# Attention maxima from queries and keys split into high and low parts instead of plain fp32 ones

## The chip, the cores and the metric

The kernel runs on one core of one Trainium2 chip, as one program. The metric is the time on the device in microseconds (us). Engine names in the profile: PE is TensorE (PEld its weight loads), DVE is VectorE, ACT is ScalarE, POOL is GpSimd, SP is SyncE, which issues DMAs.

## The reference, cut to what matters

```python
# b = 16 batches of 128 query rows, 2048 keys, 16 heads of 32
x = x + xattn(layernorm(x), ctx, ctx, wq, bq, wk, bk, wv, bv, wo, bo)
x = x + attn(layernorm(x), ...)     # causal linear attention and an MLP
x = x + ffn(layernorm(x), ...)      # linears with blockwise fp4 values

def xattn(q, k, v, wq, bq, wk, bk, wv, bv, wo, bo):
    qh, kh, vh = split into heads (q @ wq + bq), (k @ wk + bk), (v @ wv + bv)
    score = softmax(qh @ kh.T / sqrt(32), axis=-1)     # over the 2048 keys
    return (score @ vh) @ wo + bo
```

The change lies in the first line, in the cross attention. A softmax may subtract any number that is near the largest score of the row from all scores of that row. The kernel computes the scores twice: once with queries on the output partitions, to take the maximum over the keys, and once with keys on the partitions, with the maximum subtracted, for the exponential.

## The kernel before, in words

Everything is in one block with one program per engine; each engine works through its own program in order and waits on semaphores. The kernel first projects the queries of all batches and writes them to memory, and beside this it does keys, values and maxima of batch 0. Then a loop of 15 turns (`macro(i)`) handles the attention of batch i and, interleaved, projects keys and values of batch n = i+1 and finds its maxima. The last batch's attention and three later stages (self attention, MLP, and the fp4 linears) follow.

Keys of a batch are 16 pieces m = 0..15 of 128 channels (4 heads) by 512 keys; values are 16 pieces too. A turn has 16 steps s. On PE, a step has, in this order: from s = 4 on the pass for the maxima of piece m = s-4, `top` (L1178: four matmuls, one for each head, each on 32 rows of the array and on its own PSUM bank, plain fp32, 128 output rows by 512 keys); `score(i, s)` (L1187 puts the negated maximum into PSUM by a matmul of F32R operands with 512 columns on each group of 32 rows, L1192 adds the scores in fp32); `weigh(i, s-1)` (L1204, probabilities by values); and the projections `placed(s)` (L92, 12 matmuls of 512 columns each, F32R with operands split into high and low parts). Steps 0, 1 and 2 project key pieces 0, 1, 2, one each, and step 3 none; later steps have two or three. The first goes to bank 5, the next to bank 0 (with three: 5, 6, 0). `top` of pieces 12 to 15 comes after step 15. The function `top` also serves batch 0 ahead of the loop.

The other engines in a turn:
- ACT: `exp` (L981), then it copies the step's projections out of PSUM (`item`: keys L971, values L975).
- DVE: one reduction to the maximum for each head of a `top` (L1053), `gather` of the weighted values (L1062, L1065), at the end of a turn the negated maxima (`negate`), and the reciprocals of the denominators (L1083).
- POOL: for each step `add_up` sums the probabilities (L824, then L828 or L831 and L833); after steps 1, 5, 9 and 13 `split_ctx` splits a quarter of the next context into high and low parts (L909, L912); at the end of the turn it normalises (L926) and adds the bias (L918).
- SP: loads of the context, of both copies of the queries (`x_q_max`, `x_q`), stores. It issues the store of batch i's output, which waits for L918, and behind it the next turn's first context load.

The semaphore waits set the order: `await_item` holds a PSUM bank until it has been copied out, `await_maxed` until DVE has reduced it.

Of the kernel before, what the change touches and what calls it, by code (L numbers as in the profile page):

```python
# [5 lines left out]
F32 = mybir.dt.float32  # L6
# [299 lines left out]
def self_stage(nc, sc, banks, att, x, wo, bo, ln1, w_qkv, wo2, ln2, resid, y2, id_t, ones):  # L306
# [421 lines left out]
    stage.w_ready, stage.attT_lo, stage.xbo_ready, stage.y_ready = w_ready, attT_lo, xbo_ready, y_ready  # L728
    stage.qkv, stage.r_ready, stage.xm_ready = qkv, r_ready, xm_ready
    stage.r_stored, stage.z_stored = r_stored, z_stored  # L730
    return stage


def attention_phase(nc, x, wq, bq, ctx, wk, bk, wv, bv, ident, wo, bo, ln1, w_qkv, wo2, ln2,
# [8 lines left out]
    def items(s):  # L743
# [7 lines left out]
            todo = [("k", c + 1, 2 * half - 4), ("k", c + 1, 2 * half - 3)]  # L751
        return [("k", 0, DC - 1)] + todo if s == DC else todo

    def placed(s):

        todo = items(s)
        return list(zip(todo, ITEM_BANKS[len(todo)]))

    with ExitStack() as stack:
# [13 lines left out]
        recip = sc.at("x_recip", [P, D], F32, 101)  # L773
        out_t = sc.at("x_out", [P, D], F32, 103)
        id_t = sc.at("x_id", [P, P], F32, 105)
        shift_in = sc.at("x_shift_in", [P, P], F32, 105.5)
        shift = sc.at("x_shift", [P, S], F32R, 106)
        maxima = sc.at("x_maxima", [P, NKC, NH], F32, 106.5)
# [16 lines left out]
        ctx_loaded, ctx_hi, ctx_ready = sc.sem("x_ctx_loaded"), sc.sem("x_ctx_hi"), sc.sem("x_ctx_ready")  # L795
        q_max_loaded, q_loaded = sc.sem("x_q_max_loaded"), sc.sem("x_q_loaded")
        k_done, k_ready = sc.sem("x_k_done"), sc.sem("x_k_ready")
        v_done, v_ready = sc.sem("x_v_done"), sc.sem("x_v_ready")
        m_done, maxed, negated, shift_cols = (
            sc.sem("x_m_done"), sc.sem("x_maxed"), sc.sem("x_negated"), sc.sem("x_shift_cols"))  # L800
# [7 lines left out]
        q = q_stage(nc, sc, bank, x, wq, bq, q_all, id_t, raw[2])  # L808
        late = self_stage(nc, sc, bank, attT, x, wo, bo, ln1, w_qkv, wo2, ln2, resid, y2, id_t, ones)
        late.after = mlp_stage(nc, sc, bank, late, y2, w1, b1, w2, b2, w_ff, resid, x2, wq_ff, id_t)  # L810
        late.after.after = ffn_stage(nc, sc, bank, late.after, q, x2, wq_ff, out, id_t)
        FIRST, SECOND = Tile(0, 0), Tile(0, 1)

        def rows(j):
# [88 lines left out]
        @block.gpsimd  # L903
        def _(pool):
            def split_ctx(n, c):
                pool.wait_ge(ctx_loaded, START + (n * NKC + c + 1) * 16)

                await_count(pool, v_done, n * KT + (c - 1) * TPC)
                pool.tensor_tensor(ctx_t[0][:, c % 2], ctx_raw[:], one[:].to_broadcast([P, DC, KC]),  # L909
                                   ALU.mult).then_inc(ctx_hi, 1)  # L910
                pool.wait_ge(ctx_hi, START + n * NKC + (c + 1))
                pool.tensor_tensor(ctx_t[1][:, c % 2], ctx_raw[:], ctx_t[0][:, c % 2].bitcast(F32),  # L912
                                   ALU.subtract).then_inc(ctx_ready, 1)

            def add_bias(i):
                pool.wait_ge(normed, START + (i + 1))
                pool.wait_ge(stored, START + i * 16)
                pool.tensor_tensor(out_t[:].rearrange("p (g s) -> p g s", g=DC),  # L918
                                   recip[:].rearrange("p (g s) -> p g s", g=DC),
                                   bv_t[:].rearrange("p (g o) -> p g o", o=1).to_broadcast([P, DC, S]),  # L920
                                   ALU.add).then_inc(out_ready, 1)

            def normalise(i):
                pool.wait_ge(recip_ready, START + (i + 1))
                pool.wait_ge(gathered, START + (i + 1) * NS)
                pool.tensor_tensor(recip[:], acc_t[:].rearrange("p g s -> p (g s)"), recip[:],  # L926
                                   ALU.mult).then_inc(normed, 1)

            def macro(i, ahead=True):
                for s in range(NS):  # L930
                    add_up(pool, i, s)
                    if s in (1, 5, 9):
                        split_ctx(i + 1, (s + 3) // 4)
                    if ahead and s == 13:
                        split_ctx(i + 2, 0)
                normalise(i)
                add_bias(i)

            q.set_half(pool)
            pool.memset(one[:], 1.0).then_inc(set_up, 1)  # L940
            pool.memset(ones[:], 1.0).then_inc(set_up, 1)
            pool.memset(shift_in[:], 0.0).then_inc(set_up, 1)
            late.constants(pool)
            pool.wait_ge(set_up, START + 3)
            for c in range(NKC):
                q.inverse_root(pool, c)
                if c == 0:
                    pool.wait_ge(q.w_ready, START + DC)
                split_ctx(0, c)
            split_ctx(1, 0)  # L950
            pool.wait_ge(loaded, START + 32)
# [12 lines left out]
            late.after.after.gpsimd(pool)

        @block.scalar
        def _(act):
# [9 lines left out]
            def exp(i, s):  # L977
# [15 lines left out]
            def macro(i):  # L993
                copy_shift(i)
                item(i, "v", NKC - 1, TPC - 1, 5)
                for s in range(NS):
                    exp(i, s)
                    for it, b in placed(s):
                        item(i + 1, *it, b)
                for v in range(TPC - 1):  # L1000
                    item(i + 1, "v", NKC - 1, v, LAST_BANKS[v])
                copy_den(i)
# [40 lines left out]
        def _(dve):  # L1043
# [12 lines left out]
            def gather(i, s):  # L1056
# [6 lines left out]
                else:  # L1063
                    dve.wait_ge(gathered, START + i * NS + (s - DC + 1))
                    dve.tensor_tensor(acc_t[:, g], tops[:, 0, 0:S], acc_t[:, g], ALU.add).then_inc(gathered, 1)  # L1065

            def negate(n):
                dve.wait_ge(maxed, START + HG * n * NS + HG * NS)
                dve.tensor_reduce(neg_max[:], maxima[:].rearrange("p c h -> p h c"), AX.X, ALU.max,
# [22 lines left out]
            def macro(i):  # L1092
                for s in range(NS):
                    if s >= DC:
                        maximum_by_head(i + 1, s - DC, tops)
                    if s:
                        gather(i, s - 1)
                maximum_by_head(i + 1, NS - 4, tops)
                maximum_by_head(i + 1, NS - 3, scores)
                gather(i, NS - 1)  # L1100
                maximum_by_head(i + 1, NS - 2, scores)
                maximum_by_head(i + 1, NS - 1, tops)
                negate(i + 1)
                invert(i)
# [39 lines left out]
        def _(pe):  # L1144
# [16 lines left out]
            def await_item(n, kind, c, t):  # L1161

                if kind == "k":
                    pe.wait_ge(k_ready, START + n * NS + (c * DC + t + 1))
                else:
                    pe.wait_ge(v_ready, START + n * KT + (c * TPC + t + 1))

# [2 lines left out]

            def top(n, m, banks):

                c, g = divmod(m, DC)
                pe.wait_ge(k_ready, START + n * NS + (m + 1))
                if m == 0:
                    pe.wait_ge(q_max_loaded, START + (n + 1) * 16)
                for j in range(HG):
                    mm = pe.matmul(banks[:, j], q_max[rows(j), g], k_t[rows(j), g, cols(c, KC)], start=True, stop=True)  # L1178
                mm.then_inc(m_done, 1)

            def score(i, s):
# [113 lines left out]
            for c in range(NKC):  # L1295
# [8 lines left out]
                for v in range(TPC):  # L1304
                    if v == 0:
                        pe.wait_ge(q.yT_ready, START + (c + 1) * MT)
                    await_count(pe, maxed, HG * (c * DC + v))
                    top(0, c * DC + v, scores)
                    if c < NKC - 1 or v < TPC - 1:
                        if v >= 2:  # L1310
                            await_item(0, "v", c, v - 2)
# [397 lines left out]
    return stage  # L1709


def ffn_stage(nc, sc, banks, before, q, x2, wq_ff, out, id_t):

    NQ = B // MT
    g_t, u_t = ([[sc.at(f"f_{name}{n}_{k}", [P, DC, CHUNKS[n][1]], F32R, kb) for k, kb in enumerate(kbs)]
# [39 lines left out]
    w_loaded = [q.w_loaded, q.b_loaded, sc.sem("f_w_loaded2"), sc.sem("f_w_loaded3")]  # L1755
    WL0 = (START + 16, START + 16, START, START)

    x_chain, zx, x_rounded = sc.sem("f_x_chain"), sc.sem("f_zx"), sc.sem("f_x_rounded")
    xq_ready = sc.sem("f_xq_ready")
    gate, up, silu, h_ready = sc.sem("f_gate"), sc.sem("f_up"), sc.sem("f_silu"), sc.sem("f_h_ready")  # L1760
    h_chain, zh, h_grid, h_rounded = sc.sem("f_h_chain"), sc.sem("f_zh"), sc.sem("f_h_grid"), sc.sem("f_h_rounded")
    hq_ready, th, hT_hi, hT_lo = sc.sem("f_hq_ready"), sc.sem("f_th"), sc.sem("f_hT_hi"), sc.sem("f_hT_lo")
# [97 lines left out]
    def gpsimd(pool):  # L1860
# [9 lines left out]
        def step(s):  # L1870
# [8 lines left out]
            for g in range(3):  # L1879
# [4 lines left out]
                    await_count(pool, th, e1.count(3, g - 5))  # L1884
                    scaled(hq[:, e1.ring(2), cols], h[:, cols], h_scales(g)[3], zh)
                if g == 0 and s.exists():
                    pool.wait_ge(x_rounded, START + s.count(plus=1))
                    scaled(xq[:, s.ring(2)], xq[:, s.ring(2)], x_sc4[1][:], xq_ready)
                if g > 0 and e1.exists():
                    scale_back(e1, g - 1)  # L1890
# [83 lines left out]
        block_scales(dve, xn[:], [a[:] for a in x_sc4], D, x_chain, START + s.count(7))  # L1974

    def input_grid(dve, s):
        dve.wait_ge(zx, START + s.count(plus=1))
        to_grid(dve, xq[:, s.ring(2)], xn[:], x_chain, START + s.count(7, 4), x_rounded)

    def input_lo(dve, s, src):  # L1980
# [78 lines left out]
        mm.then_inc(w_turned, 1)  # L2059

    def turn_input(pe, s, dst):
        pe.wait_ge(xq_ready, START + s.count(plus=1))
        await_from(pe, xT_lo, XT0, s.count())
        for c in range(DC):
            mm = pe.transpose(dst[:, c * P:(c + 1) * P], xq[:, s.ring(2), c * P:(c + 1) * P], id_t[:])
        mm.then_inc(tx, 1)
# [126 lines left out]
```

## Time and profile before

| | us |
|---|---|
| median of 3 runs | 3591.96 (3591.79 to 3593.48) |
| the profiled execution, its own time | 3596.26 |
| its span, first to last instruction | 3594.4 |
| PE busy | 3472.0 (97%) |
| POOL busy | 2033.1 (57%) |
| DVE busy | 1785.8 (50%) |
| ACT busy | 1107.0 (31%) |

The shares are averages over stages of different kinds: the loop of 15 turns, from about 190 us to about 2361 us, and the later stages behind it. The mean granted clock of PE is 0.989 of full speed. A row of the timeline gives the start, the time, the engine, line and operation, and in brackets the idle time before it with what ended it.

### The profile page before, as it was taken

To read this page: it belongs to the slowest core of one execution; us is meant where nothing else is said; L and a number is where in the kernel's file an instruction comes from. 1 tells how busy PE (TensorE), PEld (TensorE's weight loads), DVE (VectorE), ACT (ScalarE), POOL (GpSimd) and SP (SyncE) were. 2 spreads that over 40 slices of the span, in tenths; PEclk is the share of its full clock that TensorE was granted. 3 is DMA by queue.
4 is the path that set the end of the run, shared out by engine and by line. 5 is a ranking of instruction groups with operands and counts; after the bars stand their busy time and mean duration, and the time that the engine had idled before them with its cause. 6 is when DMAs were issued, how large, how long until landed. Compare 5 with 4: busy or idle time off the path is not lost.

```text
span 3594.4 us, 77780 instructions
## 1 busy us (share of the span) xinstructions
PE 3472.0 (97%) x31956; PEld 2687.3 (75%) x31956; DVE 1785.8 (50%) x3434; ACT 1107.0 (31%) x1264; POOL 2033.1 (57%) x1174
## 2 busy tenths in 40 slices
PE   7999999999999999999999999978999899989999
PEld 5777777777777777777777777756776678878887
DVE  5323233232332332323323323276887877579997
ACT  2233333333333333333333333351112322321111
POOL 2277876868678768686687777703444410023332
PEclk9999999999999999999999999998999999999999
DMA  3211010110111101101111011021112422320000
GB/s 121 74 39 42 28 45 16 54 34 28 42 34 36 46 16 54 34 28 42 34 36 35 27 42 45 13 75 51 55 50 77 143 92 91 114 66 24 18 23 18
DMA packets 83371, 174.62 MB, mean 49 GB/s; under 512 B 7185, under 2 KB 43153, under 8 KB 73873
## 3 DMA queue, kind: packets, MB, share of 16 engines
q1 hardware_dynamic: 82512, 168.14, 14.0%
q8 instruction: 253, 4.15, 0.5%
q10 hardware_dynamic: 576, 2.10, 0.2%
q14 instruction: 30, 0.24, 0.0%
HBM read 136.39 MB, written 33.82 MB: 47 GB/s over the span
## 4 chain that ended last, share of the span: by engine, by line
PE 86%; DVE 8%; issue 2%; ACT 1%; DMA 1%; POOL 1%; SPq 0%; DVEq 0%; ACTq 0%; POOLq 0%
PE a_bank L92 61%; PE a_bank L1178 7%; PE a_bank L1204 7%; PE a_bank L1192 6%; PE a_bank L1187 2%; DVE s_rden L543 1%; ACT x_probsT L981 1%; DVE s_am L515 1%; DVE s_st L104 1%; PE a_bank L2106 1%; POOL s_rstd L412 0%; PE a_bank L1213 0%; DVE m_ff_dst L1397 0%; DVE m_hT L1605 0%; PE a_bank L2050 0%
## 5 line engine op out<-in xcount | busy, mean ns | idle before, releaser
L1053 DVE TENSOR_REDUCE x_maxima<-a_bank 128x1 f32<-128x512 f32 x960 | 593.2, 682 | 1231.1 <-PE a_bank L1178 1231.1
L92 PE MATMUL a_bank<-x_ctx,x_wk 128*128 128x512 f32 x3072 | 743.6, 396 | 2.0 <-POOL x_ctx L912 2.0
L92 PE MATMUL a_bank<-x_wv,x_ctx 128*128 128x512 f32 x3072 | 742.9, 396 | 2.5 <-DVE x_maxima L1047 2.5
L824 POOL TENSOR_TENSOR x_pairs<-x_probsT 128x1024 f32<-128x1024 f32 x240 | 572.2, 2384 | 235.0 <-ACT x_probsT L981 230.3
L92 PEld LDWEIGHTS a_bank<-x_wv,x_ctx 128*128 128x128 f32 x3072 | 565.9, 188 | 170.9 <-DVE x_maxima L1053 39.2
L92 PEld LDWEIGHTS a_bank<-x_ctx,x_wk 128*128 128x128 f32 x3072 | 565.9, 188 | 143.9 <-issue 17.1
L981 ACT ACTIVATE x_probsT<-a_bank 128x2048 f32<-128x2048 f32 x256 | 481.8, 1882 | 389.6 <-PE a_bank L1192 261.0
L975 ACT ACTIVATE x_v<-a_bank 128x512 f32<-128x512 f32 x256 | 152.9, 597 | 603.9 <-PE a_bank L92 603.9
L971 ACT ACTIVATE x_k<-a_bank,x_bk 128x512 f32<-128x512 f32 x256 | 176.2, 688 | 479.8 <-PE a_bank L92 479.8
L912 POOL TENSOR_TENSOR x_ctx<-x_ctx_raw,x_ctx 128x2048 fp32r<-128x2048 f32 x64 | 295.2, 4612 | 5.0
L1178 PE MATMUL a_bank<-x_k,x_q_max 32*128 32x512 f32 x2048 | 283.5, 633 | 10.4 <-DVE x_acc L1062 10.4
L909 POOL TENSOR_TENSOR x_ctx<-x_ctx_raw,x_one 128x2048 fp32r<-128x2048 f32 x64 | 230.5, 3601 | 103.2 <-DMA x_ctx_raw<-in_ctx 96.8
L1192 PEld LDWEIGHTS a_bank<-x_q,x_k 32*128 32x128 f32 x8192 | 276.9, 187 | 10.5 <-issue 3.3
L1204 PE MATMUL a_bank<-x_probsT,x_v 128*32 128x128 f32 x8192 | 277.6, 276 | 1.0 <-ACT x_probsT L981 1.0
L1192 PE MATMUL a_bank<-x_q,x_k 32*128 32x128 f32 x8192 | 274.6, 270 | 0.0
L831 POOL TENSOR_TENSOR x_part<-x_pairs 128x512 f32<-128x512 f32 x180 | 231.6, 1286 | 27.6 <-POOL x_pairs L824 26.7
L1204 PEld LDWEIGHTS a_bank<-x_probsT,x_v 128*32 128x32 f32 x8192 | 208.6, 110 | 42.1 <-DVE x_maxima L1053 11.8
L833 POOL TENSOR_TENSOR x_total<-x_total,x_part 128x512 f32<-128x512 f32 x180 | 230.3, 1279 | 14.1
L92 PE MATMUL a_bank<-m_w,m_hT 128*128 128x512 f32 x768 | 190.4, 398 | 15.9 <-DVE m_hT L1605 15.9
L92 PE MATMUL a_bank<-m_yT,m_w 128*128 128x512 f32 x768 | 187.6, 394 | 1.4 <-POOL m_w L1543 1.4
L92 PEld LDWEIGHTS a_bank<-m_w,m_hT 128*128 128x128 f32 x768 | 145.2, 191 | 50.1 <-DVE m_hT L1605 20.1
L92 PEld LDWEIGHTS a_bank<-m_yT,m_w 128*128 128x128 f32 x768 | 144.9, 190 | 32.7 <-POOL m_w L1543 1.9
(199 smaller groups left out, 3871.9 us busy)
## 6 DMA issues: line engine op xcount, KB each, us to landing
x_ctx_raw<-in_ctx SPq DMA_DIRECT2D x64, 1024.0 KB, 5.0
m_ff_src<-in_w_ff SPq DMA_DIRECT2D x44, 192.0 KB, 2.6
wq_ff<-m_ff_dst SPq DMA_DIRECT2D x44, 192.0 KB, 1.9
m_w_raw<-in_w SPq DMA_DIRECT2D x32, 256.0 KB, 2.9
f_w_in<-wq_ff SPq DMA_DIRECT2D x22, 256.0 KB, 2.8
q_x<-in_x SPq DMA_DIRECT2D x16, 256.0 KB, 4.1
q_all<-q_out SPq DMA_DIRECT2D x16, 256.0 KB, 2.2
x_q_max<-q_all SPq DMA_DIRECT2D x16, 256.0 KB, 5.9
```

The lines of the kernel that those rows point to most:

```text
L92: mm = pe.matmul(out, lhs[a], rhs[b], start=first and n == 0, stop=last and n == 2)
L824: eng.tensor_tensor(pairs[:], probsT[:, s % 2, :, 0:2], probsT[:, s % 2, :, 2:4], ALU.add).then_inc(paired, 1)
L831: eng.tensor_tensor(part[:], pairs[:, :, 0], pairs[:, :, 1], ALU.add).then_inc(summed, 1)
L833: eng.tensor_tensor(total[:, s % DC], total[:, s % DC], part[:], ALU.add).then_inc(added, 1)
L909: pool.tensor_tensor(ctx_t[0][:, c % 2], ctx_raw[:], one[:].to_broadcast([P, DC, KC]), ALU.mult).then_inc(ctx_hi, 1)
L912: pool.tensor_tensor(ctx_t[1][:, c % 2], ctx_raw[:], ctx_t[0][:, c % 2].bitcast(F32), ALU.subtract).then_inc(ctx_ready, 1)
L971: act.activation(k_t[:, t, cols(c, KC)], bank[:, b], ACT.Identity, bias=bk_t[:, t:t + 1]).then_inc(k_ready, 1)
L981: act.activation(probsT[:, s % 2].rearrange("p j t s -> p (j t s)"), scores.rearrange("p j n -> p (j n)"), ACT.Exp).then_inc(exped, 1)
L1053: dve.tensor_reduce(maxima[:, c, g * HG + j:g * HG + j + 1], banks[:, j], AX.X, ALU.max).then_inc(maxed, 1)
L1178: mm = pe.matmul(banks[:, j], q_max[rows(j), g], k_t[rows(j), g, cols(c, KC)], start=True, stop=True)
L1192: mm = pe.matmul(scores[:, j, cols(t, S)], k_t[rows(j), g, cols(c * TPC + t, P)], q_t[rows(j), g], start=False, stop=t == TPC - 1)
L1204: mm = pe.matmul(tops[rows(j), 0, here], v_t[:, c * TPC + t, cols(g * HG + j, DH)], probsT[:, s % 2, j, t], start=t == 0 and (s == 0 or no ...
```

## The change

In the loop, `top` multiplies split operands: the queries and keys of batch n are each held as a high part (an F32R copy) and a low part (the rest). Three products, high by high, high by low, low by high, are added in PSUM, each of four F32R matmuls on the four groups of 32 rows. Batch 0 keeps the plain fp32 pass (`first_top`).

The parts are made so. ACT writes the high part of each key piece right after it has copied the piece out of PSUM (`key_hi`), and the high part of the queries in step 1 (`query_hi`). DVE makes the low part of ten of the sixteen key pieces straight from PSUM (`key_lo` for those where `leads` holds: m < 4 or m even), and the bank is then also held for DVE. POOL makes the low part of the other six (`key_lo`, after `add_up` of the step) and of the queries (`query_lo`, after `add_up` of step 2). `top` waits for these parts; for piece 0 also for the low part of the queries. The four new semaphores take the place of three of the last stage, which uses three of an earlier stage.

```diff
+    def leads(m):
+        return m < DC or m % 2 == 0
+    def led(m):
+        return sum(leads(k) for k in range(m + 1))
...
+        k_split = [sc.at(f"x_k_split{k}", [P, DC, KC], F32R, 183 + 8 * k) for k in range(2)]
+        q_split = [sc.at(f"x_q_split{k}", [P, DC, S], F32R, 199 + 2 * k) for k in range(2)]
...
# POOL
+            def query_lo(n):
+                pool.wait_ge(q_hi, START + n)
+                pool.tensor_tensor(q_split[1][:], q_max[:], q_split[0][:].bitcast(F32),
+                                   ALU.subtract).then_inc(lo_by_pool, 1)
+            def key_lo(n, m):
+                c, g = divmod(m, DC)
+                pool.wait_ge(k_hi, START + (n - 1) * NS + (m + 1))
+                pool.tensor_tensor(k_split[1][:, g], k_t[:, g, cols(c, KC)], k_split[0][:, g].bitcast(F32),
+                                   ALU.subtract).then_inc(lo_by_pool, 1)
             def macro(i, ahead=True):
                 for s in range(NS):
                     add_up(pool, i, s)
+                    if s == 2:
+                        query_lo(i + 1)
+                    for (kind, c, g), b in placed(s):
+                        if kind == "k" and not leads(c * DC + g):
+                            key_lo(i + 1, c * DC + g)
                     if s in (1, 5, 9):
                         split_ctx(i + 1, (s + 3) // 4)
...
# ACT
+            def key_hi(n, m):
+                act.wait_ge(k_ready, START + n * NS + (m + 1))
+                act.activation(k_split[0][:, g], k_t[:, g, cols(c, KC)], ACT.Copy).then_inc(k_hi, 1)
+            def query_hi(n):
+                act.wait_ge(q_max_loaded, START + (n + 1) * 16)
+                act.activation(q_split[0][:], q_max[:], ACT.Copy).then_inc(q_hi, 1)
...
                     for it, b in placed(s):
                         item(i + 1, *it, b)
+                        if it[0] == "k":
+                            key_hi(i + 1, it[1] * DC + it[2])
+                    if s == 1:
+                        query_hi(i + 1)
...
# DVE
+            def key_lo(n, m, b):
+                dve.wait_ge(k_hi, START + (n - 1) * NS + (m + 1))
+                dve.scalar_tensor_tensor(k_split[1][:, g], bank[:, b], bk_t[:, g:g + 1],
+                                         k_split[0][:, g].bitcast(F32), ALU.add, ALU.subtract).then_inc(k_lo_first, 1)
...
                     if s:
                         gather(i, s - 1)
+                    for (kind, c, g), b in placed(s):
+                        if kind == "k" and leads(c * DC + g):
+                            key_lo(i + 1, c * DC + g, b)
...
# PE, await_item
                     pe.wait_ge(k_ready, START + n * NS + (c * DC + t + 1))
+                    if leads(c * DC + t) and not isinstance(n, int):
+                        pe.wait_ge(k_lo_first, START + (n - 1) * led(NS - 1) + led(c * DC + t))
...
             def top(n, m, banks):
+                g, lo_before = m % DC, (n - 1) * (NS - led(NS - 1) + 1) + 1
+                if leads(m):
+                    pe.wait_ge(k_lo_first, START + (n - 1) * led(NS - 1) + led(m))
+                else:
+                    pe.wait_ge(lo_by_pool, START + lo_before + m + 1 - led(m))
+                if m == 0:
+                    pe.wait_ge(lo_by_pool, START + lo_before)
+                for a, b in CUTS:
+                    for j in range(HG):
+                        mm = pe.matmul(banks[:, j], q_split[a][rows(j), g], k_split[b][rows(j), g],
+                                       start=(a, b) == CUTS[0], stop=(a, b) == CUTS[-1])
+                mm.then_inc(m_done, 1)
```

## Rows read from the trace of the kernel before

**Rows 1.** The page: busy time by engine, and the chain that ended last, by line

```profile
PE 3472.0 (97%) x31956; PEld 2687.3 (75%) x31956; DVE 1785.8 (50%) x3434; ACT 1107.0 (31%) x1264; POOL 2033.1 (57%) x1174
...
PE a_bank L92 61%; PE a_bank L1178 7%; PE a_bank L1204 7%; PE a_bank L1192 6%; PE a_bank L1187 2%; DVE s_rden L543 1%; ACT x_probsT L981 1%; DVE s_am L515 1%; DVE s_st L104 1%; PE a_bank L2106 1%; POOL s_rstd L412 0%; PE a_bank L1213 0%; DV
```

**Rows 2.** Busy time in one turn: length, PE, PEld, DVE, ACT, POOL, then the clock

```profile
1042.36:1187.06 144.70, 144.01 (x1610) 108.34 (x1609) 46.87 (x84) 51.57 (x50) 108.71 (x55) 1.00 0.11 36
```

**Rows 3.** Timeline of PE, the head of one step: start, us, line, count

```profile
1015.76 1.14 PE L1178 MATMUL a_bank<-x_k,x_q_max 32*128 32x512 f32 x8
1016.61 0.52 PE L1187 MATMUL a_bank<-x_shift,x_pick 32*128 32x512 f32 x4
1016.95 1.07 PE L1192 MATMUL a_bank<-x_q,x_k 32*128 32x128 f32 x32
```

**Rows 4.** Timeline of PE from one turn into the next

```profile
1059.96 0.51 PE L1187 MATMUL a_bank<-x_shift,x_pick 32*128 32x512 f32 x4
...
1077.92 1.14 PE L1178 MATMUL a_bank<-x_k,x_q_max 32*128 32x512 f32 x8 [0.69 <-DVE x_acc L1062]
```

**Rows 5.** Timeline of POOL over the same stretch, from the bias of the old turn

```profile
1062.58 1.04 POOL L918 TENSOR_TENSOR x_out<-x_recip,x_bv 128x512 f32<-128x512 f32 x1
...
1071.63 3.60 POOL L909 TENSOR_TENSOR x_ctx<-x_ctx_raw,x_one 128x2048 fp32r<-128x2048 f32 x1 [0.21 <-DMA x_ctx_raw<-in_ctx]
...
1079.81 2.38 POOL L824 TENSOR_TENSOR x_pairs<-x_probsT 128x1024 f32<-128x1024 f32 x1
1082.26 1.30 POOL L828 TENSOR_TENSOR x_total<-x_pairs 128x512 f32<-128x512 f32 x1
1083.70 2.40 POOL L824 TENSOR_TENSOR x_pairs<-x_probsT 128x1024 f32<-128x1024 f32 x1
```

**Rows 6.** The same two moments in the first turn and in the latest-running one

```profile
209.65 1.14 PE L1178 MATMUL a_bank<-x_k,x_q_max 32*128 32x512 f32 x8 [0.69 <-DVE x_acc L1062]
...
213.73 1.30 POOL L828 TENSOR_TENSOR x_total<-x_pairs 128x512 f32<-128x512 f32 x1
...
1512.10 1.14 PE L1178 MATMUL a_bank<-x_k,x_q_max 32*128 32x512 f32 x8 [0.70 <-DVE x_acc L1062]
...
1517.49 1.29 POOL L828 TENSOR_TENSOR x_total<-x_pairs 128x512 f32<-128x512 f32 x1
```

**Rows 7.** Source view of L1178: waits before it, whole trace (us, times)

```profile
  DVE x_acc L1062: 10.4, 15
```

**Rows 8.** Timeline: key copies on ACT, and the PE group after the second

```profile
1064.36 0.69 ACT L971 ACTIVATE x_k<-a_bank,x_bk 128x512 f32<-128x512 f32 x1 [0.91 <-PE a_bank L92]
...
1066.59 3.02 PE L92 MATMUL a_bank<-x_ctx,x_wk 128*128 128x512 f32 x12
...
1104.65 0.69 ACT L971 ACTIVATE x_k<-a_bank,x_bk 128x512 f32<-128x512 f32 x1 [2.04 <-PE a_bank L92]
...
1107.26 1.14 PE L1178 MATMUL a_bank<-x_k,x_q_max 32*128 32x512 f32 x8
```

**Rows 9.** Groups of like operations (count, busy us, mean ns): ACT, DVE, POOL

```profile
L190 ACT ACTIVATE q_yT<-a_bank 128x512 fp32r<-128x512 f32 x16 | 8.3, 610 | 0.0
...
L2027 DVE TENSOR_TENSOR f_hT<-a_bank,f_hT 128x512 fp32r<-128x512 f32 x32 | 21.9, 688 | 3.4 <-ACT f_hT L1943 2.9
...
L831 POOL TENSOR_TENSOR x_part<-x_pairs 128x512 f32<-128x512 f32 x180 | 231.6, 1286 | 27.6 <-POOL x_pairs L824 26.7
```

**Rows 10.** Timeline of PE: like matmuls behind an idle stretch and without one

```profile
24.14 13.87 PE L92 MATMUL a_bank<-q_yT,q_w 128*128 128x512 f32 x48 [5.53 <-DVE q_yT L222]
37.85 11.04 PE L92 MATMUL a_bank<-x_ctx,x_wk 128*128 128x512 f32 x48
...
187.15 3.81 PE L92 MATMUL a_bank<-x_wv,x_ctx 128*128 128x512 f32 x9 [2.48 <-DVE x_maxima L1047]
...
1056.88 2.34 PE L92 MATMUL a_bank<-x_wv,x_ctx 128*128 128x512 f32 x9
```

**Rows 11.** Stretch behind the second idle time (columns as Rows 2)

```profile
187.20:190.90 3.70, 3.70 (x11) 2.89 (x11) 0.54 (x3) 0.00 (x0) 0.00 (x0) 0.57 0.77 261
```

More of the change, by code:

```diff
@@ L730, in self_stage @@
     stage.r_stored, stage.z_stored = r_stored, z_stored
+    stage.rden_ready, stage.xu_ready, stage.u_ready = rden_ready, xu_ready, u_ready
     return stage
@@ L797, in attention_phase @@
         k_done, k_ready = sc.sem("x_k_done"), sc.sem("x_k_ready")
+        k_hi, k_lo_first, lo_by_pool, q_hi = (
+            sc.sem("x_k_hi"), sc.sem("x_k_lo_first"), sc.sem("x_lo_by_pool"), sc.sem("x_q_hi"))
         v_done, v_ready = sc.sem("x_v_done"), sc.sem("x_v_ready")
@@ L810, in attention_phase @@
         late.after = mlp_stage(nc, sc, bank, late, y2, w1, b1, w2, b2, w_ff, resid, x2, wq_ff, id_t)
-        late.after.after = ffn_stage(nc, sc, bank, late.after, q, x2, wq_ff, out, id_t)
+        late.after.after = ffn_stage(nc, sc, bank, late.after, late, q, x2, wq_ff, out, id_t)
         FIRST, SECOND = Tile(0, 0), Tile(0, 1)
@@ L982, in exp @@
                                scores.rearrange("p j n -> p (j n)"), ACT.Exp).then_inc(exped, 1)
+            def key_hi(n, m):
+                c, g = divmod(m, DC)
+                act.wait_ge(k_ready, START + n * NS + (m + 1))
[3 more added lines that the diff above has]
+                act.activation(q_split[0][:], q_max[:], ACT.Copy).then_inc(q_hi, 1)
             def copy_shift(n):
@@ L1065, in gather @@
                     dve.tensor_tensor(acc_t[:, g], tops[:, 0, 0:S], acc_t[:, g], ALU.add).then_inc(gathered, 1)
+            def key_lo(n, m, b):
+                c, g = divmod(m, DC)
+                dve.wait_ge(k_hi, START + (n - 1) * NS + (m + 1))
+                dve.scalar_tensor_tensor(k_split[1][:, g], bank[:, b], bk_t[:, g:g + 1],
+                                         k_split[0][:, g].bitcast(F32), ALU.add, ALU.subtract).then_inc(k_lo_first, 1)
             def negate(n):
@@ L1171, in top, with first_top @@
             def top(n, m, banks):
+                g, lo_before = m % DC, (n - 1) * (NS - led(NS - 1) + 1) + 1
[10 more added lines that the diff above has]
+                mm.then_inc(m_done, 1)
+            def first_top(m):
                 c, g = divmod(m, DC)
-                pe.wait_ge(k_ready, START + n * NS + (m + 1))
+                pe.wait_ge(k_ready, START + m + 1)
                 if m == 0:
-                    pe.wait_ge(q_max_loaded, START + (n + 1) * 16)
+                    pe.wait_ge(q_max_loaded, START + 16)
                 for j in range(HG):
-                    mm = pe.matmul(banks[:, j], q_max[rows(j), g], k_t[rows(j), g, cols(c, KC)], start=True, stop=True)
+                    mm = pe.matmul(scores[:, j], q_max[rows(j), g], k_t[rows(j), g, cols(c, KC)], start=True, stop=True)
                 mm.then_inc(m_done, 1)
@@ L1307, in _ @@
                     await_count(pe, maxed, HG * (c * DC + v))
-                    top(0, c * DC + v, scores)
+                    first_top(c * DC + v)
                     if c < NKC - 1 or v < TPC - 1:
@@ L1709, in mlp_stage, with ffn_stage @@
     return stage
-def ffn_stage(nc, sc, banks, before, q, x2, wq_ff, out, id_t):
+def ffn_stage(nc, sc, banks, before, done, q, x2, wq_ff, out, id_t):
     NQ = B // MT
@@ L1756, in ffn_stage @@
     WL0 = (START + 16, START + 16, START, START)
-    x_chain, zx, x_rounded = sc.sem("f_x_chain"), sc.sem("f_zx"), sc.sem("f_x_rounded")
-    xq_ready = sc.sem("f_xq_ready")
+    zx, x_rounded, xq_ready, D0 = done.rden_ready, done.xu_ready, done.u_ready, START + B
+    x_chain = sc.sem("f_x_chain")
     gate, up, silu, h_ready = sc.sem("f_gate"), sc.sem("f_up"), sc.sem("f_silu"), sc.sem("f_h_ready")
@@ L1886, in step @@
                 if g == 0 and s.exists():
-                    pool.wait_ge(x_rounded, START + s.count(plus=1))
+                    pool.wait_ge(x_rounded, D0 + s.count(plus=1))
                     scaled(xq[:, s.ring(2)], xq[:, s.ring(2)], x_sc4[1][:], xq_ready)
@@ L1976, in input_grid @@
     def input_grid(dve, s):
-        dve.wait_ge(zx, START + s.count(plus=1))
+        dve.wait_ge(zx, D0 + s.count(plus=1))
         to_grid(dve, xq[:, s.ring(2)], xn[:], x_chain, START + s.count(7, 4), x_rounded)
@@ L2061, in turn_input @@
     def turn_input(pe, s, dst):
-        pe.wait_ge(xq_ready, START + s.count(plus=1))
+        pe.wait_ge(xq_ready, D0 + s.count(plus=1))
         await_from(pe, xT_lo, XT0, s.count())
```

## The prediction

> **What bounds the kernel now.** I read the page first. PE is busy 97% of the span, and the chain that ended last runs over PE: L92 alone 61%, L1178 7% [rows 1]. Next the busy time by stretch: one turn of the loop lasts 144.7 us, PE is busy for 144.0 of it at full clock, POOL for 108.7, ACT for 51.6, DVE for 46.9 [rows 2]. So in the loop whatever PE saves or waits shows up one for one. Third, PE's timeline inside one step, for the price of the pass; last, the timelines of PE and POOL over the change of turns, because the new waits tie the one to the other there. The reader should see in them that PE waits only once in a turn, for 0.69 us, before the pass for piece 0 [rows 4], and that the wait stands at that place in all 15 turns [rows 7].
>
> **The pass itself.** A `top` starts at 1015.76 and L1187 at 1016.61: 0.85 us for four fp32 matmuls side by side [rows 3]. In its place stand twelve F32R matmuls of 512 columns, three rounds of four. Their rows are the bounds. F32R matmuls of 512 columns on the full array, each with its own weight load, come every 11.04/48 = 0.23 us [rows 10]; three rounds at that pace are 0.69 us. L1187 is one such round on four groups of 32 rows, and from its start to that of L1192 0.34 us pass (1016.61 to 1016.95) [rows 3]; three of those are 1.02 us. So a pass gains between +0.16 and -0.17 us. I take 0.69 us, +0.16: the 0.34 holds one change of stage with a weight load that nothing covers, and between the rounds of one pass there is no wait, as there is none between the 48.
>
> L1187 also shows that the four groups run side by side: 0.34 us are far less than four times 0.23 [rows 3, 10]. The Trainium skill ("TensorE: Matmul & The Clock Gate", Measured speedup vs the span model) puts packing into four row groups at 512 columns at a speedup of 3.07, not 4. By that rule, as an estimate from that page, a round would be 4 x 0.23 / 3.07 = 0.30 us, a pass 0.90 us, and each pass would lose 0.05 us; no row here shows three such rounds in succession.
>
> Of the 16 passes in a turn, fourteen (pieces 0 to 13) lie on PE's path ahead of the stretch below. With the last two DVE's reductions set the pace: they can start one pass's gain earlier, so I count 15: 15 x 0.16 = 2.4 us a turn.
>
> **The low part of the queries.** This decides. `top` for piece 0 waits for `query_lo`, and that stands in POOL's program behind `add_up` of step 2, which stands behind `split_ctx` of step 1. POOL's rows: the split runs from 1071.63 to 1079.81, then L824 to 1082.2 and L828 to 1083.56; only then comes `query_lo`, 0.14 us later as the next operation does today [rows 5], for 1.29 us, the time of a POOL subtract or add of 128x512 (L831, 1286 ns) [rows 9]. It ends at 1084.99. PE starts `top` today at 1077.92 [rows 4]: 7.1 us too late. In the first turn the same sum is 213.73 + 1.30 + 0.14 + 1.29 - 209.65 = 6.8 us, in the latest 1517.49 + 1.29 + 0.14 + 1.29 - 1512.10 = 8.1 us [rows 6]; over the 15 turns the mean of the sum is 7.2 us. A hand-over to PE comes on top; I put it at 0.2 us (estimate, from POOL's 0.14).
>
> Can POOL come earlier? Its split in step 1 started 0.21 us after it was free, held by the DMA of the context [rows 5]. That DMA is issued behind the store that waits for L918 (1062.58), and L918 behind the reciprocals and the denominators of the old turn. So this whole chain hangs on the turn's end on PE, the same as `top` does, and the distance stays. Behind the waiting `top` in PE's program stand `score(4)`, `weigh(3)` and all projections of step 4; ACT's exponential and everything else follow them. Nothing can pass, so PE stands for 0.69 + 7.4 = 8 us in each of 15 turns. That time isn't given back: PE is the bound of the other 127 us of the turn (144.7 less 1059.96 to 1077.92) [rows 2, 4], and the next turn's POOL chain starts from that end.
>
> **The clock behind that stop.** Today the clock holds at 1.00 over the turn, with 0.69 us as its longest stop [rows 2, 4]. Longer stops cost it. Behind 2.48 us of idle time nine matmuls took 3.81 us, against 2.34 us in another place: 1.5 us lost, with a granted clock of 0.57 over the stretch, which is time at 1.2 GHz in place of 2.4 [rows 10, 11]. Behind 5.53 us of idle time 48 took 13.87 us, against 11.04: 2.8 us lost [rows 10]. A stop of 8 us is nearest the second. I take 2.5 us a turn, with 0 and 3.4 us as the ends: 0 because nothing in the loop shows such a stop, 3.4 because this one is longer than either.
>
> **What ACT, DVE and POOL get besides.** ACT: 16 `key_hi` and one `query_hi` a turn at 0.61 us (L190) [rows 9], 10.4 us on 51.6; it has gaps of 2.04 us before each key copy [rows 8]. `query_hi` sits between the copy of key piece 1 and `exp(2)` and delays that by up to 0.65 us; the probabilities of step 2 are used by POOL only after the split, so it is hidden. Without that cover it would add 0.65 us a turn. DVE: 10 `key_lo` at 0.69 us (L2027, the same kind of subtract from PSUM) [rows 9], 6.9 us on 46.9. POOL: 6 `key_lo` and `query_lo`, 7 x 1.29 = 9 us on 108.7, so 118 of some 152 us.
>
> Chain for a DVE part in a late step: copy at 1104.65 + 0.69, high part 0.1 + 0.61, low part 0.1 + 0.69 = 1106.84, and the bank is needed for `top` at 1107.26 [rows 8, 9]: 0.4 us in hand. In steps 0 and 1: 1064.36 + 0.69 + 0.71 + 0.79 = 1066.55 against a projection that starts at 1066.59 [rows 8]: nothing in hand, so perhaps 0.1 us twice a turn; but this lies before the stop for `query_lo` and goes into it. The POOL parts have time: the tightest, piece 13, is made after `add_up(14)` and used after step 15, a whole step (8.9 us) later. These edits I price at 0. If a hand-over were 0.4 us longer than I think, PE would wait some 0.3 us in each of the six late steps with a DVE key part: 2 us a turn. That end I keep for the range.
>
> The renamed semaphores of the last stage and batch 0's pass change no operation: 0.
>
> **The sum.** A turn gets longer by 7.2 + 0.2 + 2.5 - 2.4 = 7.5 us; 15 turns: 112 us. On the profiled execution that is 3596.3 + 112 = 3708 us; the median of the runs lies 4.3 us below that execution, so 3592 + 112 = 3704 us.
>
> **Rivals.**
> 1. The stop comes, the clock stays up: 15 x 5.0 = 75, 3667 us. For it: 0.69 us of idle time leave the clock alone [rows 4]. Against it: both longer stops did not [rows 10].
> 2. The three rounds don't overlap with their weight loads and cost 0.34 us each: the 2.4 us of gain become 15 x 0.17 = 2.6 us of loss, 12.5 us a turn, 188 in all, 3780 us. For it: the only round of this shape took 0.34 us. Against it: that one stands alone between two waits [rows 3]. By the Trainium skill's 3.07 for four row groups (the page above) it would be halfway, 15 x 0.05 = 0.75 us of loss, some 3751 us.
> 3. The other side, faster: POOL hands over `query_lo` before PE needs it. It decides at 1077.23, when PE is free for `top` in [rows 4]. Then only the gain of 16 passes is left, 16 x 0.16 x 15 = 38, 3554 us. Against it: POOL would need to be 7.8 us ahead of where it is, and the split of 8.2 us stands before it in the order. It would hold only if I read POOL's order wrongly.
> 4. The gain and the stop cancel: it would take 0.66 us or more per pass (9.9 us over 15), where the whole pass costs 0.85 us. Almost excluded; a stop of a third of the length would do it.
>
> **How the numbers follow.** Forecast 72%; rival 1 11%; rival 2 with its halfway point 9%; rival 3 6%; rival 4 2%. A change under 0.2% (7 us) can't be told from none here. Faster 6%, same 2%, slower 92%. The forecast's own ends: clock loss 1.5 to 3.4 us, passes between 0.69 and 0.80 us, up to 1 us of late keys, lateness 6.8 to 8.1 us, which gives 6 to 10 us a turn, 3682 to 3742 us. To leave out no more than 2 in 10 I take in rival 1 and end below rival 2: 3655 to 3750 us.
>
> **What would show it.** In the profile of the changed kernel: PE idle before the first `top` of each turn for about 8 us, 15 times, released by POOL's subtract into `x_q_split`, with L824 and L828 of step 2 right ahead of it; a granted clock under 1.00 in the microseconds behind each stop, and well under 0.989 as a mean over the loop; turns of 152 us; from the start of `top` to L1187 0.7 us in late steps. The stop missing from the timeline, or `x_q_split` done before 1077, would make the prediction wrong; a pass over 0.85 us would make it wrong in size.

## The result, and the profile after

The changed kernel takes 3729.31 us (3727.17 to 3731.14, 4 runs) beside 3592.72 us of the kernel before (3591.79 to 3595.84, 4 runs): 1.0378 times as long, 95% interval 1.0360 to 1.0396, or 137 us more. The forecast was 3704 us, 112 more, within 3655 to 3750. The profiled executions' spans differ by 133.9 us (3728.3 against 3594.4).

The page of the changed kernel, the lines that answer to [rows 1]: busy time by engine, then the chain that ended last by engine and by line.

```profile
PE 3494.3 (94%) x32916; PEld 2752.6 (74%) x32916; DVE 1900.0 (51%) x3584; ACT 1265.3 (34%) x1519; POOL 2163.7 (58%) x1279
...
PE 75%; DVE 9%; POOL 6%; issue 6%; ACT 2%; DMA 1%; SPq 0%; POOLq 0%; ACTq 0%; DVEq 0%
PE a_bank L92 54%; PE a_bank L1235 6%; PE a_bank L1272 6%; PE a_bank L1260 5%; POOL x_pairs L837 3%; PE a_bank L1255 2%; DVE x_maxima L1095 2%; POOL x_ctx L922 2%; ACT x_probsT L1010 1%; DVE s_rden L543 1%; POOL x_total L841 1%; DVE s_st L1
```

POOL is now on the chain: its sums (L837, L841) and its context split (L922). The lines of PE are now L1235 for the pass, L1255, L1260 and L1272 for what were L1187, L1192 and L1204.

One turn of the loop (stretch view: length, PE, PEld, DVE, ACT, POOL, clock), and the two stretches at its head, the stop and what follows:

```profile
1126.00:1134.80 8.80, 1.53 (x52) 1.14 (x44) 1.04 (x2) 2.46 (x2) 8.72 (x5) 0.71 0.35 119
1134.80:1141.00 6.20, 6.19 (x83) 5.17 (x84) 2.77 (x5) 1.88 (x1) 3.91 (x3) 0.58 0.01 3
1048.23:1201.83 153.60, 146.01 (x1678) 113.09 (x1678) 54.45 (x94) 62.08 (x68) 117.57 (x63) 0.97 0.10 34
```

A turn lasts 153.6 us, not 144.7 [rows 2]: 8.9 us more, in 15 turns 133 us, which is the whole difference of the spans. PE is idle for 7.6 us of a turn, where it was 0.7, and the granted clock is 0.58 in the stretch behind the stop (most of it at 1.2 GHz of the two levels, 1.2 and 2.4), where it was 1.00. The timeline over the change of turns, all engines but PEld, answers to [rows 4, 5]:

```profile
1110.26 0.51 PE L1255 MATMUL a_bank<-x_shift,x_pick 32*128 32x512 f32 x4
...
1112.40 1.04 POOL L931 TENSOR_TENSOR x_out<-x_recip,x_bv 128x512 f32<-128x512 f32 x1
...
1121.69 3.60 POOL L922 TENSOR_TENSOR x_ctx<-x_ctx_raw,x_one 128x2048 fp32r<-128x2048 f32 x1
...
1125.38 4.53 POOL L925 TENSOR_TENSOR x_ctx<-x_ctx_raw,x_ctx 128x2048 fp32r<-128x2048 f32 x1
...
1129.86 2.34 POOL L837 TENSOR_TENSOR x_pairs<-x_probsT 128x1024 f32<-128x1024 f32 x1
...
1132.28 1.26 POOL L841 TENSOR_TENSOR x_total<-x_pairs 128x512 f32<-128x512 f32 x1
1133.50 1.26 POOL L944 TENSOR_TENSOR x_q_split<-x_q_max,x_q_split 128x512 fp32r<-128x512 f32 x1
...
1134.81 1.65 PE L1235 MATMUL a_bank<-x_k_split,x_q_split 32*128 32x512 f32 x12 [7.29 <-POOL x_q_split L944]
1136.26 0.63 PE L1255 MATMUL a_bank<-x_shift,x_pick 32*128 32x512 f32 x4
...
1136.69 1.91 PE L1260 MATMUL a_bank<-x_q,x_k 32*128 32x128 f32 x32
```

Read it from the bottom: L1260 takes 1.91 us, where it took 1.07 in [rows 3]; the pass before it waited 7.29 us for `query_lo`, which came behind the sums of step 2 and they behind the context split, back to back. The tile view of `x_q_split` counts who waited for it (us, times): the stop stands in all 15 turns, 7.3 us on average.

```profile
  PE a_bank L1235: 109.3, 15
```

A late step without a stop answers to [rows 3]:

```profile
1048.23 0.97 PE L1235 MATMUL a_bank<-x_k_split,x_q_split 32*128 32x512 f32 x12
1049.08 0.50 PE L1255 MATMUL a_bank<-x_shift,x_pick 32*128 32x512 f32 x4
1049.41 1.05 PE L1260 MATMUL a_bank<-x_q,x_k 32*128 32x128 f32 x32
```

From the pass to the negated maximum 0.85 us, from the pass to the scores 1.18 us. They were 0.85 and 1.19 us. Here is the surprise: the pass of split operands is worth next to nothing.

### The profile page after: what moved, and what is told of

The parts are those of the page before. It is cut to its first block, busy times and chain, and to the rows that moved or that the text cites. A ratio compares the mean times of both kernels' runs of the same rounds, so it can differ in the third digit from the quotient of the medians.

```text
span 3728.3 us, 80372 instructions
## 1 busy us (share of the span) xinstructions
PE 3494.3 (94%) x32916; PEld 2752.6 (74%) x32916; DVE 1900.0 (51%) x3584; ACT 1265.3 (34%) x1519; POOL 2163.7 (58%) x1279
## 4 chain that ended last, share of the span: by engine, by line
PE 75%; DVE 9%; POOL 6%; issue 6%; ACT 2%; DMA 1%; SPq 0%; POOLq 0%; ACTq 0%; DVEq 0%
PE a_bank L92 54%; PE a_bank L1235 6%; PE a_bank L1272 6%; PE a_bank L1260 5%; POOL x_pairs L837 3%; PE a_bank L1255 2%; DVE x_maxima L1095 2%; POOL x_ctx L922 2%; ACT x_probsT L1010 1%; DVE s_rden L543 1%; POOL x_total L841 1%; DVE s_st L104 1%; POOL x_q_split L944 1%; DVE s_am L515 1%; PE a_bank L2174 0%
## 5 line engine op out<-in xcount | busy, mean ns | idle before, releaser
L92 PE MATMUL a_bank<-x_wv,x_ctx 128*128 128x512 f32 x3072 | 742.7, 396 | 8.6 <-DVE x_maxima L1095 6.1
L92 PE MATMUL a_bank<-x_ctx,x_wk 128*128 128x512 f32 x3072 | 742.4, 396 | 2.2 <-POOL x_ctx L925 2.2
L837 POOL TENSOR_TENSOR x_pairs<-x_probsT 128x1024 f32<-128x1024 f32 x240 | 572.5, 2385 | 282.7 <-ACT x_probsT L1010 282.7
L92 PEld LDWEIGHTS a_bank<-x_wv,x_ctx 128*128 128x128 f32 x3072 | 566.1, 188 | 171.5 <-DVE x_maxima L1095 26.1
L92 PEld LDWEIGHTS a_bank<-x_ctx,x_wk 128*128 128x128 f32 x3072 | 564.8, 188 | 144.2 <-issue 23.5
L1112 DVE SCALAR_TENSOR_TENSOR x_k_split<-a_bank,x_bk,x_k_split 128x512 fp32r<-128x512 f32 x150 | 112.6, 750 | 615.0 <-ACT x_k_split L1016 615.0
L1235 PE MATMUL a_bank<-x_k_split,x_q_split 32*128 32x512 f32 x2880 | 242.8, 441 | 109.4 <-POOL x_q_split L944 109.3
L1260 PEld LDWEIGHTS a_bank<-x_q,x_k 32*128 32x128 f32 x8192 | 290.6, 195 | 8.9
L1272 PE MATMUL a_bank<-x_probsT,x_v 128*32 128x128 f32 x8192 | 286.5, 282 | 1.0 <-ACT x_probsT L1010 1.0
L1260 PE MATMUL a_bank<-x_q,x_k 32*128 32x128 f32 x8192 | 287.4, 279 | 0.0
L922 POOL TENSOR_TENSOR x_ctx<-x_ctx_raw,x_one 128x2048 fp32r<-128x2048 f32 x64 | 230.5, 3602 | 96.0 <-DMA x_ctx_raw<-in_ctx 90.0
L1235 PEld LDWEIGHTS a_bank<-x_k_split,x_q_split 32*128 32x128 f32 x2880 | 125.4, 191 | 203.7 <-POOL x_q_split L944 113.4
L1272 PEld LDWEIGHTS a_bank<-x_probsT,x_v 128*32 128x32 f32 x8192 | 216.1, 113 | 38.9 <-DVE x_maxima L1095 9.0
L92 PE MATMUL a_bank<-m_w,m_hT 128*128 128x512 f32 x768 | 188.9, 395 | 17.7 <-DVE m_hT L1673 17.7
L92 PE MATMUL a_bank<-m_yT,m_w 128*128 128x512 f32 x768 | 187.3, 394 | 1.5 <-POOL m_w L1611 1.5
```

The lines of the kernel that those rows point to most:

```text
L92: mm = pe.matmul(out, lhs[a], rhs[b], start=first and n == 0, stop=last and n == 2)
L837: eng.tensor_tensor(pairs[:], probsT[:, s % 2, :, 0:2], probsT[:, s % 2, :, 2:4], ALU.add).then_inc(paired, 1)
L1235: mm = pe.matmul(banks[:, j], q_split[a][rows(j), g], k_split[b][rows(j), g], start=(a, b) == CUTS[0], stop=(a, b) == CUTS[-1])
L1260: mm = pe.matmul(scores[:, j, cols(t, S)], k_t[rows(j), g, cols(c * TPC + t, P)], q_t[rows(j), g], start=False, stop=t == TPC - 1)
L1272: mm = pe.matmul(tops[rows(j), 0, here], v_t[:, c * TPC + t, cols(g * HG + j, DH)], probsT[:, s % 2, j, t], start=t == 0 and (s == 0 or no ...
```

## The experiments

Times stand beside the kernel before, measured together with them: 3593.64 us for the first four, 3591.39 for the next four, 3594.86 for the last two. Ratios are to these.

**The stop taken away.** On POOL:

```diff
-                    if s == 2:
+                    if s == 1:
                         query_lo(i + 1)
```

> The changed kernel with the low part of the queries made on POOL after add_up of step 1, ahead of the context split, in place of after step 2. Theory A (the whole loss is the stop before the first pass of a turn, with the clock that falls behind it, and the new pass is worth nothing on PE): the stop goes back to about 0.7 us, the granted clock stays 1.00 in the loop, a turn lasts 144.5 to 145 us, and the time is 3585 to 3600 us, no different from the kernel before. Rival B (the new pass does gain 0.16 us, and something else in the loop eats it): about 3554 us once the stop is gone. Rival C (key parts on DVE and ACT cost PE time all over the turn): 3610 us or more with no stop in the trace.

Measured: 3597.92 us, ratio 1.0016 (1.0007 to 1.0025). A turn lasts 144.7 us again, the loop's clock has no drop, and before the first pass of a turn PE waits 0.79 us, for DVE (stretch view, and the wait in the source view of L1235, us and times):

```profile
1000.00:1144.70 144.70, 143.58 (x1675) 111.12 (x1674) 54.40 (x94) 61.96 (x67) 117.75 (x62) 1.00 0.11 36
...
  DVE x_acc L1104: 11.8, 15
```

So the stop with what hangs on it is the whole loss (theory A), and B and C fall. By the ratio some 6 us remain over; the profiled execution, the fastest of the eleven (span 3591.9 us), doesn't show them, and their cause is open.

**The stop filled.** Ahead of PE's wait:

```diff
                 if m == 0:
+                    for _ in range(28):
+                        pe.matmul(bank[:, 7], wv_t[0][:, 0, 0:P], wv_t[1][:, 0], start=True, stop=True)
                     pe.wait_ge(lo_by_pool, START + lo_before)
```

> The changed kernel with 28 matmuls of 512 columns that do nothing of use, on constant weights into a bank that is free, ahead of PE's wait for the low part of the queries (6.6 us of the 7.3 us stop). Theory A (the fallen clock costs 2 to 2.3 us a turn on top of the stop): the clock stays 1.00, a turn lasts 151.3 to 151.7 us, the time falls by 30 to 35 us to 3695 to 3700 us. Rival D (the clock is not the cause, the stretch behind the stop is slow for another reason, such as exp that comes late): the time stays at 3725 to 3735 us.

Measured: 3699.86 us, ratio 1.0289 (1.0271 to 1.0307), by the ratios 32 us less than the changed kernel; rival D is out. PE waits as long for `query_lo`, but busy:

```profile
1113.90 6.63 PE L1233 MATMUL a_bank<-x_wv,x_wv 128*128 128x512 f32 x28 [0.69 <-DVE x_acc L1104]
1120.98 0.98 PE L1237 MATMUL a_bank<-x_k_split,x_q_split 32*128 32x512 f32 x12 [0.45 <-POOL x_q_split L944]
...
1122.01 1.07 PE L1262 MATMUL a_bank<-x_q,x_k 32*128 32x128 f32 x32
...
1000.00:1151.50 151.50, 149.71 (x1693) 115.81 (x1689) 53.94 (x94) 62.02 (x67) 117.31 (x62) 1.00 0.10 34
```

The scores take 1.07 us again, the clock over the turn (last row, stretch view) is 1.00, and a turn lasts 151.3 us. The fallen clock thus costs 2.3 us a turn (153.6 less 151.3), the stop itself 6.6 us (151.3 less 144.7).

**The old pass with all the new waits.** In `top`:

```diff
-                for a, b in CUTS:
-                    for j in range(HG):
-                        mm = pe.matmul(banks[:, j], q_split[a][rows(j), g], k_split[b][rows(j), g], ...)
+                c = m // DC
+                for j in range(HG):
+                    mm = pe.matmul(banks[:, j], q_max[rows(j), g], k_t[rows(j), g, cols(c, KC)], start=True, stop=True)
```

> The changed kernel with the old pass, four plain fp32 matmuls, but with all the parts still made by ACT, DVE and POOL and all the new waits kept. Theory A (the split pass is worth 0): 3725 to 3735 us, as the changed kernel. Rival B (the split pass gains 0.16 us at each of 240 passes): 3729 + 36 = 3765 us.

Measured: 3730.45 us, ratio 1.0382 (1.0366 to 1.0398). The stop is the same:

```profile
1137.49 2.09 PE L1235 MATMUL a_bank<-x_k,x_q_max 32*128 32x512 f32 x8 [7.29 <-POOL x_q_split L944]
```

The split pass against the fp32 pass, all else equal, is worth nothing that can be measured; rival B is out. That leaves why.

**One product of three.** `q_split[0]` by `k_split[0]` alone, with the early `query_lo`.

> As e1_query_first, but the pass has only the product of the high parts (it leaves out the two products with low parts, so its maxima are less exact): one round of four matmuls in place of three. Theory A1 (PE itself is the limit in the pass: a weight load that nothing covers, then 0.234 us a round): from the start of the pass to L1187's successor 0.35 to 0.4 us, 12 steps gain 0.45 us each, a turn lasts some 138 us and the time is 3500 to 3515 us. Theory A2 (score waits behind the pass for ACT's copy of bank 0, which ends 0.7 to 0.8 us after the start of the pass): it stays 0.7 to 0.85 us, a step gains under 0.1 us, and the time is 3570 to 3590 us.

Measured: 3578.74 us, ratio 0.9962 (0.9949 to 0.9975). The timeline of PE in a late step:

```profile
1005.43 0.51 PE L1234 MATMUL a_bank<-x_k_split,x_q_split 32*128 32x512 f32 x4
1006.28 0.51 PE L1253 MATMUL a_bank<-x_shift,x_pick 32*128 32x512 f32 x4 [0.34 <-ACT x_v L1004]
```

The pass is over in 0.51 us, and still 0.85 us pass before L1253: PE is idle for 0.34 us and is released by ACT's copy of bank 0, into which `score` writes. A2 holds. The 15 us come in the main from the two pairs of passes at the turn's end, which have no `score` between them: each pair takes 1.36 to 1.38 us up to the next line, against 1.95 us before. The two pass lengths also give the pace of the rounds: (0.97 - 0.51) / 2 = 0.23 us.

**Half of that copy left out, with each of three passes** (fp32 here, three products next, one product in e8_high_only_short_copy). These three kernels leave out half of the copy of each key or value piece in bank 0, so their output is not the reference's. In ACT's loop, for the projection in bank 0:

```diff
                     for it, b in placed(s):
-                        item(i + 1, *it, b)
+                        item(i + 1, *it, b, KC // 2 if b == 0 else KC)
```

> The kernel before, with one thing left out: in the loop ACT copies only the first 256 of the 512 columns of each projection that lies in bank 0 (the output is not the reference's). That lets score wait about 0.27 us less for bank 0: the copy should end some 0.57 us after the start of the pass, not 0.8. Theory A2 (two limits lie on one another: the fp32 pass itself, 0.85 us, and that copy): nothing moves, from the start of the pass to L1187 it stays 0.85 us, 3588 to 3596 us. Rival (the copy alone is the limit): each of 12 steps loses 0.25 us, 3545 to 3555 us.

Measured: 3593.65 us, ratio 1.0006 (0.9997 to 1.0016). The negated maximum starts earlier (0.64 us behind the start of the pass), the scores don't: 1.19 us as before. So the fp32 pass by itself also holds the scores there, and the copy is no limit of its own.

```profile
1013.19 1.14 PE L1186 MATMUL a_bank<-x_k,x_q_max 32*128 32x512 f32 x8
1013.83 0.74 PE L1195 MATMUL a_bank<-x_shift,x_pick 32*128 32x512 f32 x4
1014.39 1.07 PE L1200 MATMUL a_bank<-x_q,x_k 32*128 32x128 f32 x32
```

> e1_query_first (three products, no stop) with the same part left out: ACT copies only half the columns of each projection in bank 0. Theory A2 (the split pass is shorter than 0.85 us on PE, but score behind it is held by the copy of bank 0): the pass falls to what PE needs, three rounds of 0.234 us, 0.70 us to L1187, 12 steps gain 0.15 us, a turn lasts 143 us and the time is 3565 to 3575 us. Theory A1 (PE needs 0.81 us or more, since the first weight load is not covered): at most 0.04 us a step, 3587 to 3597 us.

Measured: 3570.51 us, ratio 0.9946 (0.9930 to 0.9963), which by the ratios is 25 us less than e1_query_first.

```profile
1002.78 0.97 PE L1243 MATMUL a_bank<-x_k_split,x_q_split 32*128 32x512 f32 x12
1003.59 0.41 PE L1263 MATMUL a_bank<-x_shift,x_pick 32*128 32x512 f32 x4
1003.82 1.06 PE L1268 MATMUL a_bank<-x_q,x_k 32*128 32x128 f32 x32
```

From the pass to the scores 1.04 us, 0.15 less than with the fp32 pass and the same short copy; so the split pass does need 0.15 us less of PE, and only the copy hides it. A2 holds by the time and the turn (143.0 us). Its 0.70 us up to the negated maximum was 0.81, though, as A1 had it; the gain shows one operation later.

**High parts alone.** No `key_lo`, no `query_lo`, one product; `top` waits for `k_hi` and `q_hi`.

> The changed kernel with the product of the high parts alone and no low parts at all: no key_lo, no query_lo, and the pass waits for the high parts only (the maxima are a little off; a softmax may subtract any number near the maximum). Theory A: as e4_one_product, the steps keep 0.85 us from the pass to L1187 because of the copy of bank 0, the double passes at the turn's end are shorter; 3570 to 3582 us, 10 to 20 us below the kernel before. Rival C (the parts made on DVE and POOL cost time of their own): 3560 us or less.

Measured: 3573.03 us, ratio 0.9946 (0.9930 to 0.9963), as forecast. Against e4_one_product the ratio is 0.0016 lower, 6 us, and the two intervals overlap: making the low parts costs little, so C is small.

> e7_high_only with half the copy of each projection in bank 0 left out. Theory A2: the pass itself needs only 0.34 us, so the whole shortening of the copy shows, to L1187 0.57 us in place of 0.85, 12 steps gain 0.28 us, the turn falls by 3.4 us and the time is 3520 to 3535 us. Theory A1 (something else than that copy holds score): 3570 to 3582 us, as e7_high_only.

Measured: 3538.31 us, ratio 0.9852 (0.9836 to 0.9869); the turn falls from 143.1 to 140.9 us. A shorter copy now shows: 0.63 us from the pass to the negated maximum (0.85 with the full copy, expected 0.57), as theory A2 says, with 35 us in place of the 50 that its 12 x 0.28 us in 15 turns make; the time lies 3 us outside its range.

```profile
1008.76 0.51 PE L1229 MATMUL a_bank<-x_k_split,x_q_split 32*128 32x512 f32 x4
1009.39 0.51 PE L1248 MATMUL a_bank<-x_shift,x_pick 32*128 32x512 f32 x4
```

**The copy covered by order, nothing left out of it.** From e7_high_only, on PE: in the projection of bank 0, and ahead of `score`:

```diff
                     for d in range(DC):
+                        if d == 2 and midway:
+                            midway()                  # the pass of the next step
...
+                    if s > DC:
+                        pe.wait_ge(exped, START + i * NS + s)
+                        await_maxed(n, s - DC, 1)
+                        weigh(i, s - 1)
```

> e7_high_only with PE's order in the late steps changed so that ACT's copy of bank 0 is covered: the pass for the next step stands in the middle of the second projection (behind 6 of its 12 matmuls), and weigh of the step before comes ahead of score. Behind the copy then lie half a projection and 1.0 us of weigh. Theory A2: a step takes 5.67 us of projections, 0.1 us for going back to them, 0.34 us of pass, 1.0 us of weigh and 1.34 us of score, 8.45 us in place of 8.86; 11 steps and 15 turns gain 65 us, 3500 to 3515 us. Rival (breaking up the projection costs as much as it gives, or exp comes too late behind the later score): 3560 us or more.

Measured: 3535.77 us, ratio 0.9837 (0.9823 to 0.9850): the fastest of all that copy everything, 1.6% below the kernel before. By the ratios it gained 39 us on e7_high_only where 65 were expected, between theory and rival:

```profile
1007.29 0.51 PE L1225 MATMUL a_bank<-x_k_split,x_q_split 32*128 32x512 f32 x4
1007.73 1.66 PE L92 MATMUL a_bank<-x_ctx,x_wk 128*128 128x512 f32 x6
1009.31 1.08 PE L1261 MATMUL a_bank<-x_probsT,x_v 128*32 128x128 f32 x32
1010.32 0.51 PE L1244 MATMUL a_bank<-x_shift,x_pick 32*128 32x512 f32 x4
1010.66 1.06 PE L1249 MATMUL a_bank<-x_q,x_k 32*128 32x128 f32 x32
1011.65 4.38 PE L92 MATMUL a_bank<-x_ctx,x_wk 128*128 128x512 f32 x18
1015.96 0.51 PE L1225 MATMUL a_bank<-x_k_split,x_q_split 32*128 32x512 f32 x4
```

PE has no idle time left in such a step, which is 8.67 us (expected 8.45): 24 matmuls of projection take 1.58 + 4.31 = 5.89 us when broken up, against 5.66 us in one piece, and the way back from the pass 0.10 us (0.44 us to the projection, less 0.34). I had counted only the second.

> e1_query_first with the same change of order and all three products. The split pass needs 0.70 us on PE (e6_split_short_copy), going back to the projection 0.1 us: theory A2 gives 8.8 us a step in place of 8.855, a gain of about 10 us, 3578 to 3592 us. Rival: DVE's key parts, which now stand in the way of an earlier pass, hold it, 3600 us or more.

Measured: 3751.68 us, ratio 1.0440 (1.0424 to 1.0455): the rival's side, 150 us above the 3600 us at which it began.

```profile
1012.75 0.97 PE L1239 MATMUL a_bank<-x_k_split,x_q_split 32*128 32x512 f32 x12 [1.06 <-DVE x_k_split L1112]
1013.65 1.66 PE L92 MATMUL a_bank<-x_ctx,x_wk 128*128 128x512 f32 x6
```

In steps with key pieces bank 5 is held until DVE has made the low part, and the earlier pass waits 1.06 us for it. All 11 steps also pay for the broken projection and 0.90 us of pass. A turn lasts 155.1 us, 10.4 more than with e1_query_first: six times 1.05 and eleven times 0.3 us (9.16 us a step with values, against 8.85) make 9.6 of them.

## Why the prediction was right, and where it was off

- **The stop for `query_lo`** was foreseen with its place and cause. Forecast 7.4 us a turn on top of 0.69, measured 7.29 us of idle time in all, a growth of 6.6 us. The forecast was 0.8 us too large. POOL's L931 (L918 before) now starts 2.14 us behind the first negated maximum of the turn, not 2.62 us [rows 4, 5]; there PE waits 0.30 us for DVE just ahead (L92 at 1107.20). And the two hand-overs, put at 0.14 and 0.2 us, took next to nothing: L944 starts at 1133.50, when L841 ends, and PE 0.05 us behind the end of L944. That taking the stop away gives 3598 us shows the cause.
- **It is not given back**: right. With the stop filled, the turn still grew by 6.6 us.
- **The clock**: forecast 2.5 us, measured 2.3 us by filling the stop. Rival 1 (no loss of clock) is out.
- **The gain of the pass, 15 x 0.16 = 2.4 us a turn**: this term failed, it was 0. Its price on PE was near, 0.15 us by e6_split_short_copy, and so was the pace of 0.23 us a round. The error is in the sentence that fourteen passes "lie on PE's path": `score` behind the pass also waits for ACT's copy of bank 0, and that ends 0.8 us after the pass starts. It could have been read in the trace of the kernel before (timeline behind the pass of 1107.26 [rows 8]):

```profile
1107.37 0.69 ACT L971 ACTIVATE x_k<-a_bank,x_bk 128x512 f32<-128x512 f32 x1 [2.03 <-PE a_bank L92]
...
1108.11 0.19 PEld L1187 LDWEIGHTS a_bank<-x_shift,x_pick 32*128 32x128 f32 x4 [0.54 <-ACT x_k L971]
```

  The weight loads of L1187 are released by that very copy, 0.05 us behind its end. I checked the copies only against the next `top`. The sum with 0 in this place, less the 1.0 us by which stop and clock were too large (7.4 + 2.5 against 6.6 + 2.3), is 8.9 us a turn, 133 us. The two errors partly cancel, so that the total came within 25 us is in part luck. Of the signs named, one failed for the same reason: 0.7 us from `top` to L1187 stayed 0.85.
- **Rival 2** (0.34 us a round): out, the rounds come at 0.23 us. The Trainium skill's 3.07 for four row groups ("TensorE: Matmul & The Clock Gate", Measured speedup vs the span model) would by the prediction's estimate make a round 0.30 us; here, in rounds that follow on one another, it is 0.23 us, as fast as one matmul on the full array [rows 10]. The measurement decides.
- **The parts on ACT, DVE and POOL at 0**: right within what e7_high_only shows. A DVE part took 0.75 us, not 0.69, an ACT part 0.63, not 0.61; the 0.4 us in hand in late steps bore that.
- **Rival 3** (faster) is out; its condition, `query_lo` in time, was made in e1_query_first, and even then the 38 us of gain that it named weren't there. Rival 4 (gain and stop cancel) is out too.

## What to carry to other kernels

A new operand that is made by another engine costs what stands ahead of it in that engine's order: look for the first consumer, and put the maker ahead of the long work, not behind it. Before you shorten a stage on the busiest engine, list each wait of the stage behind it and when its releaser ends: two limits of the same length (here a pass of some 0.85 us and a copy that ends 0.8 us behind its start) hide one another, and only shortening both pays: 0 us for either alone, 25 us for both. If a value needs to be near, not exact, as the maximum in a softmax, try it from the high parts alone: here 0.5% below the kernel before, 1.6% with the pass moved.

## What the runs showed of the hardware

- With the copy out of the way, the scores start 1.19 us behind the start of four fp32 matmuls of 512 columns on four row groups (e5_fp32_short_copy), and 1.04 us behind that of the three F32R rounds in their place (e6_split_short_copy). So twelve F32R matmuls in place of four fp32 ones gain 0.15 us. The rounds follow one another every 0.23 us.
- Idle time of 7.3 us on PE cost 2.3 us a turn beyond itself, at a granted clock of 0.58 behind it; 28 matmuls of no use in its place brought those back (e2_filled_stop, clock 1.00).
- Breaking a run of 24 full-array matmuls once for a pass on row groups cost 0.23 us in the run itself, besides 0.10 us behind the pass (e9_high_only_moved).
